# The first normalised rows of seven layers are made at the end of the layer ahead of each

## What is computed

```python
def _layernorm(x, axis=-1, eps=1e-05):
    m = jnp.mean(x, axis=axis, keepdims=True)
    v = jnp.var(x, axis=axis, keepdims=True)
    return (x - m) / jnp.sqrt(v + eps)
...
    x = x + _L0_attn_ref(_layernorm(x, axis=-1), ...)
    x = x + _L0_xattn_ref(_layernorm(x, axis=-1), ctx_768, ...)
    x = x + _L0_ffn_ref(_layernorm(x, axis=-1), ...)
```

## Time and profile before

| | us |
|---|---|
| median of 3 runs | 2229.15 (2228.09 to 2235.91) |
| profiled execution | 2220.46 |
| its span, first to last instruction | 2218.7 |
| TensorE busy in the span | 1955.1 (88%) |
| VectorE busy | 1398.9 (63%) |
| ScalarE busy | 1114.9 (50%) |
| GpSimd busy | 679.5 (31%) |
| mean granted TensorE clock | 0.922 of full |

### The profile page before, as it was taken

The page is one execution under the profiler, slowest core; times in us unless marked ns, Lnnn a source line. Parts: engine busy times, 40 slices in busy tenths (PEclk is TensorE's granted clock), DMA queues, the critical chain, the costliest instruction groups (busy, mean ns, idle before and its releaser), DMA issues. The chain is left out here.

```text
span 2218.7 us, 37310 instructions
## 1 busy us (share of the span) xinstructions
PE 1955.1 (88%) x12447; PEld 1163.5 (52%) x12447; DVE 1398.9 (63%) x3181; ACT 1114.9 (50%) x2823; POOL 679.5 (31%) x972
## 2 busy tenths in 40 slices
PE   6779999989996889866999998887999999699996
PEld 3434454434443455644666666565666666244443
DVE  6468889655452665576666665675666665567673
ACT  5325555544431467343555554442666666167763
POOL 7444432111102541300111110733433332523312
PEclk9859999989998799977999999996999999699997
DMA  1043231097661331001000000101000000443321
GB/s 43 14 100 87 48 87 44 2 222 174 154 154 35 89 88 39 25 10 38 1 1 1 1 1 1 39 23 45 1 1 1 1 1 1 107 90 82 79 54 31
DMA packets 116907, 111.96 MB, mean 50 GB/s; under 512 B 55877, under 2 KB 93552, under 8 KB 114416
## 3 DMA queue, kind: packets, MB, share of 16 engines
q1 hardware_dynamic: 78832, 91.76, 17.1%
q0 software_dynamic: 4608, 16.78, 2.9%
q10 hardware_dynamic: 33280, 1.05, 0.7%
HBM read 93.36 MB, written 15.20 MB: 49 GB/s over the span
## 5 line engine op out<-in xcount | busy, mean ns | idle before, releaser
L1081 DVE TENSOR_REDUCE L_xattn_mx<-L_xattn_psS 128x1 f32<-128x512 f32 x512 | 326.4, 684 | 123.1 <-PE L_xattn_psS L1213 118.8
L1323 ACT ACTIVATE L_xattn_PT<-L_xattn_psT 128x512 f32<-128x512 f32 x512 | 283.2, 599 | 96.1 <-PE L_xattn_psT L1225 90.3
L708 ACT ACTIVATE L_attn_pr<-L_attn_psS,L_attn_negm 128x256 f32<-128x256 f32 (+1 forms) x512 | 222.5, 447 | 52.5 <-PE L_attn_psS L619 33.6
L1213 PE MATMUL L_xattn_psS<-L_xattn_KR,L_xattn_QR 72*128 72x512 bf16 x512 | 212.8, 421 | 37.4 <-DMA L_xattn_QR<-L_xattn_q_parts 21.3
L488 DVE TENSOR_REDUCE L_attn_negm<-L_attn_psS 128x2 f32<-128x512 f32 x256 | 165.0, 687 | 117.6 <-PE L_attn_psS L609 117.5
L1225 PE MATMUL L_xattn_psT<-L_xattn_QR,L_xattn_KR 75*128 75x256 bf16 x1024 | 197.9, 278 | 4.4 <-DMA L_xattn_QR<-L_xattn_mp 2.0
L1239 PE MATMUL L_xattn_psO<-L_xattn_PT,L_xattn_V 128*32 128x256 f32 x2048 | 191.3, 395 | 3.1 <-ACT L_xattn_PT L1323 1.1
L609 PE MATMUL L_attn_psS<-L_attn_qk 64*128 64x256 f32 x1024 | 146.2, 403 | 9.5 <-ACT L_attn_pr L708 9.5
L2243 DVE TENSOR_TENSOR L_ffn_act<-L_ffn_act,L_ffn_cwb 128x512 f32<-128x512 f32 x128 | 85.7, 689 | 101.0 <-ACT L_ffn_act L2408 88.1
L413 POOL TENSOR_TENSOR L_attn_qk<-L_attn_rotc,L_attn_rots 128x512 f32<-128x512 f32 x64 | 81.2, 1268 | 209.9 <-DVE L_attn_rotc L476 163.8
L2408 ACT ACTIVATE L_ffn_act<-L_ffn_psU 128x512 f32<-128x512 f32 (+1 forms) x132 | 78.5, 597 | 131.9 <-PE L_ffn_psU L2339 128.1
(11 more groups left out here) (610 smaller groups left out, 3895.7 us busy)
## 6 DMA issues: line engine op xcount, KB each, us to landing
L_xattn_KR<-L_xattn_k_parts SPq DMA_DIRECT2D x96, 192.0 KB
L_ffn_cwb<-L_ffn_weights_by_expert SPq DMA_DIRECT2D x32, 512.0 KB, 11.4
L_ffn_cwb<-L_ffn_weights_by_expert POOLq DMA_DIRECT2D x32, 512.0 KB, 10.6
L_xattn_QR<-L_xattn_q_parts SPq DMA_DIRECT2D x32, 288.0 KB
L_xattn_k_parts<-L_xattn_ks SPq DMA_DIRECT2D x48, 128.0 KB, 2.4
L_attn_QR<-L_attn_q_parts SPq DMA_DIRECT2D x16, 288.0 KB
L_attn_KR<-L_attn_k_parts SPq DMA_DIRECT2D x48, 96.0 KB
L_xattn_q_parts<-L_xattn_qs SPq DMA_DIRECT2D x48, 64.0 KB, 2.1
```

The source lines that it names most:

```text
L708: ins = nc.scalar.activation(pr[n % 3][:, r, t, 0:width], psS[(2 * n + r) % 3][:, t, 0:width], ACT.Exp, bias=negm[:, n % 4, t, r:r + 1], a ...
L1081: nc.vector.reduce_max(mx[:, b % 2, u, hd:hd + 1], psS[n % 2][:], AX.X).then_inc(s_used, 1)
L1213: ins = nc.tensor.matmul(psS[n % 2][:, i * keys:(i + 1) * keys], QR[b % NB][0:PAIR, hd, t * P:(t + 1) * P], KR[b % NB][0:PAIR, hd, :], sta ...
L1323: nc.scalar.activation(PT[n % NPT][:, 2 * u:2 * u + 2], psT[i % NPS][:], ACT.Exp).then_inc(exp_ready, 1)
```

## The change

A buffer first_h of four tiles, with statistics, moments and roots of its own and four semaphores, is allocated once for the whole model. Three functions fill it: first_moments and first_rows on VectorE, first_roots on GpSimd. Layers 0, 1, 2, 4, 5, 9 and 10 call them near the ends of their lists, for as many tiles as NORM_AHEAD says, once their own update of those tiles of x has been made. The layers behind them (1, 2, 3, 5, 6, 10, 11) leave out the norm of their first group, and their transposes read first_h without a wait. In layer 5 the quantising of the first group moves ahead of the moments of the other twelve tiles, and ScalarE's first size ahead of its copies of turned weights. The other diff lines adapt counts of semaphores.

```diff
+        self.first_h = self.sb("first_h", [P, 4, D], F32)
...
+    def first_turn(self):
+        return sum(1 for n in LAYERS if n in NORM_AHEAD and n <= self.at)
+
+    def first_moments(self, dve):
+        if self.at in NORM_AHEAD:
+            tiles = range(NORM_AHEAD[self.at])
+            before = sum(NORM_AHEAD[n] for n in LAYERS if n in NORM_AHEAD and n < self.at)
+            for t in tiles:
+                self.nc.vector.bn_stats(self.first_stats[:, t], self.x[:, t // TB, t % TB]).then_inc(self.first_chain, 1)
+            dve.wait_ge(self.first_chain, before + len(tiles))
+            for t in tiles:
+                self.nc.vector.bn_aggr(self.first_mom[:, t], self.first_stats[:, t]).then_inc(self.first_var, 1)
+
+    def first_roots(self, pool):
+        if self.at in NORM_AHEAD:
...
+            self.nc.gpsimd.tensor_scalar(self.first_veps[:, 0:n], self.first_mom[:, 0:n, 1], LN_EPS, None, ALU.add).then_inc(self.first_eps, 1)
+            pool.wait_ge(self.first_eps, self.first_turn())
+            self.nc.gpsimd.tensor_tensor(self.first_rstd[:, 0:n], self.first_veps[:, 0:n], self.half[:, 0:n], ALU.pow).then_inc(self.first_root, 1)
+
+    def first_rows(self, dve):
+        if self.at in NORM_AHEAD:
+            dve.wait_ge(self.first_root, self.first_turn())
+            for t in range(NORM_AHEAD[self.at]):
+                self.nc.vector.tensor_scalar(self.first_h[:, t], self.x[:, t // TB, t % TB], self.first_mom[:, t, 0:1], self.first_rstd[:, t:t + 1],
+                                             ALU.subtract, ALU.mult)
...
+NORM_AHEAD = {0: 2, 1: 4, 2: 2, 4: 4, 5: 2, 9: 2, 10: 4}
...
             link(nc.gpsimd.memset(eps[:], LN_EPS))
-            norm(0)
-            pool.wait_ge(h_ready, TB)
             nc.gpsimd.memset(V[0][:], 1.0).then_inc(v_set, 1)
             norm(1)
-            pool.wait_ge(h_ready, 2 * TB)
+            pool.wait_ge(v_set, 1)
+            pool.wait_ge(h_ready, TB)
...
-            moments(0)
             moments(1)
...
+                if n == NH - 8:
+                    await_read(dve, ("O", 1, NO - 1))
+                    m.first_moments(dve)
+                if n == NH - 2:
+                    m.first_rows(dve)
...
                 if kind == "T":
-                    pe.wait_ge(h_ready, TB * (b + 1))
+                    wait(pe, h_ready, TB * b)
...
-                        ins = nc.tensor.transpose(bank[:, t * P:(t + 1) * P], h[:, t], m.ident[:])
+                        ins = nc.tensor.transpose(bank[:, t * P:(t + 1) * P], (h if b else m.first_h)[:, t], m.ident[:])
...
-            dve_moments(nc, link, norms[0], xs[:GT], D, LN_EPS).then_inc(moments, 1)
-            negated(0)
-            dve_moments(nc, link, norms[1], xs[GT:], D, LN_EPS).then_inc(moments, 1)
+            normalise("x", 0)
+            dve_moments(nc, link, w, xs[GT:], D, LN_EPS).then_inc(moments, 1)
+            levels("x", 0)
+            negated()
             dve.wait_ge(h_ready, GT)
-            normalise("x", 0)
-            negated(1)
-            levels("x", 0)
-            dve.wait_ge(h_ready, 2 * GT)
             normalise("x", 1)
...
-            for b in range(B - 2, B):
-                update(b)
+            dve.wait_ge(x_done, 1)
+            m.first_moments(dve)
+            update(B - 2)
+            m.first_rows(dve)
+            update(B - 1)
...
             nc.scalar.activation(warm[:], m.half[:, 0:1], ACT.Silu)
+            size("x", 0)
             act.wait_ge(w_turned, 1)
...
-            rows_h(0)
-            size("x", 0)
             rows_h(1)
...
+            dve.wait_ge(x_done, 1)
+            m.first_moments(dve)
             gated(3)
             after_mixer(3)
+            m.first_rows(dve)
             update(2)
...
-            find_moments(0)
             find_moments(1)
-            normalise(0)
             dve.wait_ge(w_loaded, 32)
...
+                if n == N:
+                    dve.wait_ge(x_done, 1)
+                    m.first_moments(dve)
+                if n == N + 6:
+                    m.first_rows(dve)
...
+                if n == NN - 2:
+                    await_read(dve, ("O", 0, TB - 1))
+                    m.first_moments(dve)
+                if n == NN + 3:
+                    m.first_rows(dve)
...
+                if n == NT:
+                    dve.wait_ge(x_done, 2 * TB)
+                    m.first_moments(dve)
+                if n == NT + 2:
+                    m.first_rows(dve)
```

More of the change, by code:

```diff
@@ L446, in find_moments @@
             def find_moments(b):
-                wait(dve, moments, b)
+                wait(dve, moments, b - causal)
                 for t in range(TB):
@@ L551, in run @@
                 if kind == "T":
-                    if b == 0:
+                    if b == 0 and not causal:
                         pe.wait_ge(first_h, TB)
-                    else:
+                    if b > 0:
                         pe.wait_ge(h_ready if causal else hi_ready, TB * b)
@@ L1045, in moments @@
             def moments(b):
-                wait(dve, var_ready, b)
+                wait(dve, var_ready, b - 1)
                 for t in range(TB):
@@ L1409, in _ @@
         def _(pool):
-            for i, w in enumerate(norms):
-                pool.wait_ge(moments, i + 1)
-                pool_rsqrt(nc, m, w, w.n).then_inc(rstd, 1)
+            pool.wait_ge(moments, 1)
+            pool_rsqrt(nc, m, w, w.n).then_inc(rstd, 1)
+            m.first_roots(pool)
         @block.vector
```

104 lines of the change are left out of this document (56 added, 48 removed).

## The result

The changed kernel took 2218.99 us (median of 7 runs), the kernel before 2230.83 (7 runs) beside it: a ratio of 0.9937, interval 0.9915 to 0.9959, or 11.8 us less. Two later comparisons of the same two programs gave 0.9956 (0.9936 to 0.9976) and 0.9946 (0.9922 to 0.9970). The forecast was 11.9 us less and 2217.3. The profiled execution took 2204.23, 16.2 less than that of before. The medians are 11.8 apart, so some 4 us of that belong to these two executions and not to the kernels.

The account below looks back on a forecast made before the run. At layer borders nothing of the old layer covers the new one's first norm, so TensorE idles. Seven head gains less 0.5 us for layer 4's tail sum to 11.9 us, from 2229.15 to 2217.3; range 2209 to 2228.

Parts of the forecast that it names:

- (d): Rival, chance 0.06: heads wait for loads and tables in any case, only layers 5 and 11 gain; 3 us, 2226.
- Border 1|2: Start of layer 2: first transpose moves ahead, affinities then wait for the second router load; 2.4 us gained (1.2 to 3.0).
- Border 2|3: Start of layer 3: transpose moves ahead, q's product then waits for a plain load; 1.95 us gained (1.5 to 2.3).
- Border 4|5: Start of layer 5: quantisation starts at the border, up products come after ScalarE's rows; 2.25 us gained (1.4 to 3.4).
- Border 9|10: Start of layer 10: same code as layer 1's start, q's split begins earlier; 1.5 us gained (0.3 to 1.5).
- Border 0|1: Start of layer 1: q's split and first scores earlier, V's fill moved ahead of K's cast; 1.75 us, 0.65 if cast stays long.
- Border 5|6: Start of layer 6: ScalarE copies turned rows right after its table and weight scaling; 1.35 us gained (0.7 to 1.5).
- Border 10|11: Start of layer 11: first product gains nothing, second group's rows no longer wait for GpSimd's root; 1.2 us (0 to 1.3).
- Layer 4's tail: End of layer 4: added moments, roots and four rows delay the last update; cost 0.5 us (0.2 to 1.1).
- (a): Rival, chance 0.24: partial gain, VectorE's cast still held and the clock rises when it does now; 6.5 us, 2222.7.
- (b): Rival, chance 0.12: less idle time ahead of long streams ends TensorE's slow clock sooner; 5 us more, 2212.3.
- (c): Rival, chance 0.06: slow stretches of three attention ramps grow by 14 us each, 21 us lost, 11.9 won; 2238.

Follow-up runs that it names:

- e_411: Changed kernel with only layers 5 and 11 taking their first rows from the layer ahead, other five borders as before; ratio 0.9992 to the kernel before.
- n_before: The kernel before, run and traced once more unchanged; ratio 1.0025 (1.0005 to 1.0045) against itself.
- e_copy_first: Changed kernel, but in layer 5 ScalarE copies the first transpose before making the second group's rows; ratio 0.9940 to the kernel before.
- e_hold: Changed kernel, but in layers 1, 3 and 10 GpSimd fills V between its norm's root and rows; one execution, layer 1's cast took 0.99 us.
- e_tails: Changed kernel, but only the tails: seven layers make first_h, every layer still makes its own first norm; ratio 1.0006 to the kernel before.
- e_rest: Changed kernel with only borders 0|1, 1|2, 2|3, 5|6 and 9|10, layers 5 and 11 starting as before; ratio 0.9984 to the kernel before.
- e_pad: Changed kernel with an unused third slot in q's DRAM buffer of layers 1, 3 and 10; one execution, layer 1 at 341.2 us.
- e_ext: Changed kernel with layer 5's copy ahead of ScalarE's rows, and layer 3 making layer 4's first two tiles; ratio 0.9941 to the kernel before.

## Why the prediction was right, point by point

**The time.** 2217.3 forecast, 2218.99 measured; 11.9 us forecast, 11.8, 11.4 and 9.1 in three comparisons. That is 0.63%, 0.44% and 0.54%, so just at the bound, as the text had put it. The kernel before stood 1.7 us higher in this comparison (2230.83) than in the one the forecast started from (2229.15), which is why the time is 1.7 off and the difference 0.1. That the difference fits to 0.1 us is luck: single terms missed by up to 0.9, both ways, as the first updates show (in layers 1, 2, 3, 5, 6, 10 and 11 they give 1.1, 2.3, 1.9, 1.9, 2.2, 1.6 and 1.6 us for 1.75, 2.4, 1.95, 2.25, 1.35, 1.5 and 1.2 forecast). The gains of layers 6, 10 and 11 stand above the upper bounds that the text gave them (1.5, 1.5 and 1.3). Two slips change no term: TensorE idled some 5 us ahead of the first transposes of layers 2, 3 and 11 only (5.46, 5.38, 4.89), but 3.91 in layer 6 and 2.4 in layers 1 and 10; and (d) with 3 us added ends at 2229, not 2228.

**What bounds the starts, and the ceiling of a norm.** Right. In layers 2 and 3 the load named comes last, in layer 5 ScalarE's rows, in layer 6 its table.

**The terms that held.** Border 1|2: 2.4 forecast, 2.4 at the affinities and 2.3 in the layer's length. Border 2|3: 1.95 forecast, 2.2 at q's product, 2.4 at the scores, 1.9 at the first update; the 4.5 of the layer's length is no measure of it. Border 4|5: 2.25 forecast, 2.0 at the up products and the same 2.0 in the length of e_411, where the stretches of half clock at the layer's start are as long as in n_before and come 2.0 us sooner; e_copy_first shows that the rows of ScalarE, the reason given, were what came last. Border 9|10: 1.5 forecast, 1.7 at the scores, 1.6 at the first update. The layer as a whole didn't get shorter (302.5 against 301.9 us in the mean): it moves by 8 us behind its first update, and the text's sign that the span gets shorter by the term can't be seen there.

**Border 0|1: 1.75 forecast.** The chain was right: q's split 1.65 to 1.86 us sooner, the cast short, the fill its cause (e_hold). The step that failed is the silent one, that the scores follow q's split at the old distance. The regrouping in between took 7.5 to 10.3 us. At the scores the mean gain is 0.9, in the layer's length 1.1, and 0.3 and 0.4 without the trace of e_tails. A second step was left open in the text, that the end of the slow clock moves with the work. In all 14 traces the length of layer 1 is half the time of its first scores plus half the time at which the half clock ends, both from the barrier, plus 306.0 to 306.2 us. That end lies at 57.2 us in before and 57.1 in e_rest, whose scores came 1.1 us sooner and whose layer was 0.6 shorter: where the end stays, half of a gain at the scores is kept. It came at 57.1 to 58.6 in seven of the nine traces with the new start and 3 us sooner in two (e_pad, e_ext), which took 341.2 and 341.7 us.

**Border 5|6: 1.35 forecast, 2.2 measured.** The copy came 1.4 us sooner, as said. The rest goes with the clock, of which the text took only what follows the work: where the half clock ends at nearly the same time, 8.3 us behind the barrier in e_tails (old start) and 7.8 in e_rest (new one), the first updates of x stand 1.0 us apart, and the other 1.2 come with its earlier end in the others. The first 10 us of layer 6, columns as above, before:

```profile
1041.08:1051.08 10.00, 6.37 (x14) 3.78 (x16) 2.16 (x11) 3.55 (x6) 4.35 (x9) 0.50 0.74 208
```

and after:

```profile
1030.05:1040.05 10.00, 7.57 (x26) 4.97 (x27) 2.72 (x7) 3.71 (x7) 3.33 (x7) 0.67 0.74 208
```

The half clock ends 8.3 to 10.1 us behind the barrier in the traces with the old start and 5.8 to 7.8 with the new one. What TensorE did before it rose: it idled 3.91 us ahead of its transpose in before, and 1.33 ahead of it and 1.72 behind it in after.

**Border 10|11: 1.2 forecast, 1.6 measured.** The wait for GpSimd's root is gone. The first product was to gain nothing, and it came at 5.4 to 5.5 us in eight of ten traces where it was 5.7 to 5.9: in after the scale was there 4.1 us behind the barrier, and VectorE was free to take it.

**Layer 4's tail: 0.5 forecast, 0.3 measured** in the tail itself, within the bounds of 0.2 to 1.1. The other 0.6 of this layer lies in its start and goes by the end of the slow clock; whether the tail moves that end is open (e_tails).

**Rivals.** (d) is refuted by e_411. (a) is refuted in its first half: the cast is not held (0.56 us in layer 1 in every kernel with the fill in front). (b) and (c) named the clock. Of (c)'s long ramps there is none: the slow stretch of layer 1 lasts 55 to 58 us with the old start and 51 to 55 with the new one (51 in two traces of nine). (b) is true in small: layer 3's slow stretch ends 47.4 to 51.4 us behind the barrier with the old start and 45.1 to 48.5 with the new one, layer 6's as above, and layer 6 gains more than its chain. But other layers move as much without a change to their starts (8: 54.1 to 67.7 us, 0: 97.1 to 103.9, and 97.5 to 103.6 in one program), which the text had listed as a sign of being wrong. That sign was ill chosen: it speaks of the execution, not of the kernel.
